# Two-layer block, MoE routing of the second layer placed inside the selective scan: one change to a Trainium2 kernel

## The chip, the cores and the metric

The kernel runs on one core of a Trainium2 chip. Its time is device microseconds of the execution, median of several runs. The core has a matrix engine (TensorE, PE in the profile, with PEld for its weight loads), VectorE (DVE), ScalarE (ACT), GpSimd (POOL), and SyncE (SP), which only issues transfers. Each engine works through its own instruction list in order and meets the others at semaphores; 16 DMA engines move the data. The profile counts from the start of the span of one profiled execution.

## What is computed

Two transformer-like layers on 4 batches of 1024 rows of 128 values (4096 tokens, float32). Layer 0 is causal attention and a mixture of experts; the change doesn't touch it. Layer 1 is a Mamba-style selective scan and a mixture of experts with a fixed capacity. The parts of layer 1 that matter here:

```python
# selective scan, per batch: over 1024 steps, 128 channels x 16 states
h = a_t * h + bu_t
y_t = jnp.einsum('bdn,bn->bd', h, c_t)

# experts, called once with every token's best expert and once with its second:
tpe = jnp.bincount(top_expert, length=NUM_EXPERTS)
indices = jnp.argsort(top_expert)
xe = jnp.where(valid[..., None], xf[tok_idx], 0.0)      # at most 512 tokens for each of 8 experts
h = jax.nn.gelu(jnp.einsum('ech,ehf->ecf', xe, w1), approximate=True)
ye = jnp.einsum('ecf,efh->ech', h, w2)
out = jnp.zeros((tokens + 1, hs), xf.dtype).at[tok_safe.reshape(-1)].add(ye.reshape(-1, hs))
```

Before each part the rows are layer-normalized and scaled and shifted by values made from a condition vector. Between the scan and the experts stand the norm, the scores (normed rows times an 128x8 router matrix), the choice of the best and of the second expert, and each token's slot: how many earlier tokens chose the same expert.

## The kernel before

Everything stays in SBUF as 32 tiles of 128 tokens; batch b owns tiles 8b to 8b+7 (`TPB` is 8). The stages of layer 1 are blocks of the program, one after the other, with a meeting of all engines between two blocks.

**The scan** (`selective_scan`) runs batch by batch. A batch has 16 groups of 8 channels; group (b, g) is a recurrence over 128 partitions and 1024 columns, done in two halves of 512. `scan_plan` writes one list of steps, and every engine walks through this one list in its order and does its own part of each step, so the list sets the order on all engines. For a group VectorE makes products in PSUM (`product`, `m_ps_bu`, L1993, twice) and two scans (`first_half` L2001, `second_half` L2007, both to `m_st`). ScalarE makes the decay `m_da` three groups ahead (L2153). GpSimd multiplies the state by C (`m_hc` or `attn_t`, L2171); the results stand in NHC = 8 buffers, and the states in 4 (`NST_BUF`). TensorE sums four groups at once (step `sum`, L1970 and L1973, queued two groups behind). SyncE brings the spread inputs (`m_x_rep`). Beside that, `prepare(b + 1)` puts the next batch's input steps (norm, turn, conv, u, z, raw, soft, rep, delta) beside groups 0 to 11 of batch b; the Silu steps load another table on ScalarE, and the step `table` (L2103) loads the first one again. The preceding batch's results are multiplied by z on GpSimd (L2183), put out and added to x beside groups 3 and 4 (step `out`, L1958, L1959, L2118), and their row statistics are made by VectorE beside groups 5 and 6 (step `stats`, L156, L160). Transposes and the like share two PSUM banks `ps_w`, in turn.

**The norm block** (`Norm`, "ln3") then normalizes all 32 tiles: GpSimd every fourth, VectorE the others, with scale and shift by rows as separate instructions (L212, L217, L219), TensorE transposes (L262) and makes the scores (L282), ScalarE copies (L229). Meanwhile SyncE loads the second layer's weights w2 and w1, 2 MB each (L2489, L2490).

**The experts' block** (`capacity_experts`) begins with `Dispatch`: on VectorE the choice of the best expert, running counts, slots, then the second expert and its slots and weights (L1111 to L1164), with two small TensorE products for the counts. GpSimd sends the 32 tiles of normed rows to their slots in DRAM by indirect DMAs (L2372), first all 32 of the first choice, then splits w1 into a high and a low part (`Split.gpsimd`, L305, 8 instructions, each after ScalarE's copy L299), then sends the 32 of the second. SyncE waits for all 32 sends of a choice and fetches expert after expert (L2393). TensorE handles 16 expert blocks (8 experts, two choices): transposes `c_tr`, L2262, products up (`c_up`) and down (`c_dn`, L2286). GpSimd gathers the results (L2383) once the 8 blocks of a choice are stored, and VectorE mixes them and adds them to x.

## Time and profile before

| | |
|---|---|
| Median of 3 runs | 1915.2 us (1911.8 to 1917.24) |
| Profiled execution | 1911.14 us, span of the core 1909.3 us |
| Busy over the span | PE 1554.6, DVE 1198.2, ACT 773.3, POOL 1264.3 us |
| Layer 0 | up to about 1371 us |
| Scan | 1371 to 1640.5 us |
| Norm block | 1640.8 to 1673.5 us |
| Experts' block | 1673.8 us to the end |

A row of a timeline is: start in us, duration in us, engine, line, operation, output<-inputs, shape, and how many instructions the row merges; brackets give the idle time before it and what ended it. A line is that of the kernel before. "issue" is time of no wait that the profile shows. The shares of busy time over the whole span say little here, since the change lies in three stages of the last 540 us.

### The profile page before, as it was taken

The numbers are of one execution on the slowest core, as the hardware profiler recorded it, in microseconds if no ns is written. First come the engines' busy times: TensorE is split into PE (matmuls) and PEld (weight loads), VectorE is DVE, ScalarE is ACT, GpSimd is POOL, SyncE is SP. The second block draws the span as 40 slices with busy tenths as digits, with TensorE's granted clock in tenths as the row PEclk, the third lists the DMA queues.
The fourth block names the chain that finished last, engine by engine and source line by source line (L and its number), as shares of the span: only waits on it lengthen the run. The fifth ranks groups of instructions, "written<-read, shape, count | busy, mean of one in ns | idle before, by whom it ended". The sixth has DMA issues, their size and how long they took to land. (4 is left out here: it accounts for less than half of the span.)

```text
span 1909.3 us, 26415 instructions
## 1 busy us (share of the span) xinstructions
PE 1554.6 (81%) x8848; PEld 1070.2 (56%) x8848; DVE 1198.2 (63%) x2522; ACT 773.3 (40%) x1294; POOL 1264.3 (66%) x1080
## 2 busy tenths in 40 slices
PE   5799999999999999999999999999875553517960
PEld 3455555756566665557566587888622211417850
DVE  6876676566666666765665065666589999732224
ACT  2245444354443454443444542322387663113320
POOL 5588898788887888987897842110047766368446
PEclk7799999999999999999999999999978777558985
DMA  6233221121213112211211020000065554213323
GB/s 174 67 78 84 62 67 34 45 67 36 65 36 78 34 40 62 68 34 45 67 42 26 13 63 1 1 1 1 24 165 145 147 151 119 91 38 105 97 65 86
DMA packets 93543, 125.29 MB, mean 66 GB/s; under 512 B 13648, under 2 KB 53476, under 8 KB 93408
## 3 DMA queue, kind: packets, MB, share of 16 engines
q1 hardware_dynamic: 89312, 115.58, 24.2%
q0 software_dynamic: 4096, 8.02, 1.5%
q8 instruction: 72, 1.18, 0.3%
q14 instruction: 63, 0.52, 0.1%
HBM read 56.56 MB, written 16.78 MB: 38 GB/s over the span
## 5 line engine op out<-in xcount | busy, mean ns | idle before, releaser
L835 DVE CUSTOM_DVE_ANT_0 ring<-ring,mask 128x128 f32<-128x128 f32 (+7 forms) x512 | 383.7, 769 | 185.3 <-PE ring L697 184.9
L921 ACT ACTIVATE prob<-ring 128x512 f32<-128x512 f32 x576 | 315.2, 598 | 297.0 <-PE ring L712 293.5
L975 POOL TENSOR_TENSOR acc<-acc,prob 128x512 f32<-128x512 f32 x272 | 353.1, 1298 | 72.8 <-ACT prob L921 48.9
L728 PE MATMUL ps_o<-prob,v 128*64 128x256 f32 x2304 | 281.5, 386 | 4.1 <-issue 3.8
L697 PE MATMUL ring<-k,x 128*128 128x512 f32 (+3 forms) x768 | 249.5, 404 | 37.7 <-ACT prob L921 22.1
L711 PE MATMUL ring<-x,k 128*128 128x512 f32 x576 | 257.7, 447 | 24.9 <-DVE neg_m L835 15.7
L712 PE MATMUL ring<-x,k 128*128 128x512 f32 x576 | 229.0, 398 | 0.0
L697 PEld LDWEIGHTS ring<-k,x 128*128 128x128 f32 x768 | 136.3, 197 | 145.1 <-ACT prob L921 50.5
L728 PEld LDWEIGHTS ps_o<-prob,v 128*64 128x64 f32 x2304 | 153.9, 136 | 106.0 <-issue 38.3
L972 POOL TENSOR_TENSOR acc<-prob 128x512 f32<-128x512 f32 x144 | 184.4, 1281 | 8.2 <-ACT prob L921 6.8
L942 POOL TENSOR_TENSOR other<-other,sin 128x512 f32<-128x512 f32 x96 | 136.3, 1420 | 58.4 <-DVE other L814 57.8
L711 PEld LDWEIGHTS ring<-x,k 128*128 128x128 f32 x576 | 109.2, 190 | 99.9 <-issue 43.6
L944 POOL TENSOR_TENSOR rot<-rot,other 128x512 f32<-128x512 f32 x96 | 129.2, 1346 | 7.5
L1681 POOL TENSOR_TENSOR first_h<-first_h,e_scaled 128x512 f32<-128x512 f32 x8 | 10.2, 1271 | 176.2 <-DVE e_scaled L1563 176.2
L712 PEld LDWEIGHTS ring<-x,k 128*128 128x128 f32 x576 | 109.8, 191 | 19.5 <-issue 6.9
L827 DVE TENSOR_TENSOR rot<-rot,other 128x512 fp32r<-128x512 f32 x64 | 73.1, 1142 | 69.5 <-ACT other L903 69.5
L1549 DVE TENSOR_TENSOR e_both<-e_silu,ps_moe 128x512 f32<-128x512 f32 x88 | 60.4, 686 | 87.1 <-PE ps_moe L1389 68.7
L2171 POOL TENSOR_TENSOR attn_t<-m_st,m_crep 128x1024 f32<-128x1024 f32 x32 | 75.3, 2358 | 55.8 <-DVE m_st L2007 49.0
L1633 ACT ACTIVATE e_silu<-ps_moe 128x512 f32<-128x512 f32 x88 | 52.6, 598 | 136.7 <-PE ps_moe L1389 133.9
L960 POOL TENSOR_SCALAR_AFFINE_SELECT prob<-prob 128x512 f32<-128x512 f32 x128 | 91.3, 713 | 24.8 <-ACT prob L921 23.7
L2383 POOL DMA_INDIRECT c_got<-slots_out,d_slot x64 | 64.8, 1012 | 63.1 <-DMA slots_out<-wo 44.2
L813 DVE TENSOR_TENSOR rot<-ring,cos 128x512 f32<-128x512 f32 x96 | 66.3, 690 | 59.2 <-PE ring L679 58.8
(301 smaller groups left out, 3050.8 us busy)
## 6 DMA issues: line engine op xcount, KB each, us to landing
x<-other SPq DMA_DIRECT2D x256, 128.0 KB, 2.4
m_x_rep<-u_mem SPq DMA_DIRECT2D x59, 512.0 KB, 4.6
x<-rot SPq DMA_DIRECT2D x128, 128.0 KB, 2.3
slots_in<-zeros SPq DMA_DIRECT2D x2, 2048.0 KB, 8.7
slots_out<-wo SPq DMA_DIRECT2D x16, 256.0 KB, 2.5
gate<-slots_in SPq DMA_DIRECT2D x11, 256.0 KB, 3.2
m_x_rep<-u_mem SPq DMA_DIRECT2D x10, 256.0 KB, 4.4
e_w<-in_w SPq DMA_DIRECT2D x3, 704.0 KB, 6.6
```

The source lines that it names most:

```text
L697: mm = e.matmul(ps[:, c0:c1], x1[g % 2][:, h, qs], k1[g % 3][:, c0:c1], start=True, stop=True)
L711: e.matmul(banks(step, BANK), k1[g % 3][:, ks], x1[g % 2][:, :, qs], start=True, stop=False)
L712: e.matmul(banks(step, BANK), k2[g % 3][:, ks], x2[g % 2][:, :, qs], start=False, stop=True).then_inc(s2_pe.sem, 1)
L728: mm = e.matmul(ps_o[s * D:(s + 1) * D, qb % 2 * 2 * P:(qb % 2 + 1) * 2 * P], v[g % 2][:, kb, :], prob[i % NPROB][:, s * 2 * P:(s + 1) * 2 ...
L835: e.tensor_tensor_reduce(ps, ps, mask_1[:, SEQ - n:SEQ], 1.0, -3.0 * NEG, ALU.add, ALU.min, neg_m[g % 2][:, c, h, qb % QPC:qb % QPC + 1]). ...
L921: e.activation(prob[i % NPROB][:, :], banks(("s2",) + key, BANK), ACT.Exp, scale=-1.0).then_inc(s2_exp.sem, 1)
L942: e.tensor_tensor(other[i][:, :], other[i][:, :], sin[:, cc], ALU.mult).then_inc(rotated.sem, 1)
L944: e.tensor_tensor(rot[i][:, :], rot[i][:, :], other[i][:, :], ALU.add).then_inc(rotated.sem, 1)
L960: e.affine_select(tile[:, :], tile[:, :], [[0, G], [1, P]], ALU.is_ge, 0.0, base=0, channel_multiplier=-1).then_inc(causal.sem, 1)
L972: e.tensor_tensor(total[:, :], first[:, :], tile[:, :], ALU.add).then_inc(summed.sem, 1)
L975: e.tensor_tensor(total[:, :], total[:, :], tile[:, :], ALU.add).then_inc(summed.sem, 1)
L2171: e.tensor_tensor(hc[(b * NG + g) % NHC][:, :], st[r][:, :], crep[b % 2][:, :], ALU.mult).then_inc(hc_pool.sem, 1)
```

## The change

The norm block is gone, and with it `Dispatch`. Its work up to the slots of the first choice is cut by batches and put as new steps into the scan's list (`routed`): batch b's statistics as before, then `rstd3` (two ACT, then five DVE instructions), `norm3` (ACT; scale and shift rows on POOL, for the last batch's first half on DVE), `turn3` and `score` (PE, ACT), `choose`, `count`, `place` (DVE, PE, DVE), beside the groups of batch b+1, and `send` (POOL), two tiles beside each of groups 2 to 5 of batch b+2. For batch 2 `count`, `place` and the sends come after the last group; for batch 3 all of it but the sends, which the experts' block begins with. The small DVE instructions are handed out one at a time between the big ones of a group (`between`); after the last group they go at once. `SecondChoice` does the second choice for all tokens at the experts' start. The loads of w1 (now two halves) and w2 are issued at the start of the experts' block. The `m_hc` buffers shrink from 8 to 6 since the normed rows `h` need the room, `h_t` holds two batches instead of four, and the zeroing of `c_got` moves to the second expert block.

```diff
+    def choose(self, e, b, scored):
+        c, shape, slots = self.chain, [P, TPB, NE], float(NE * CAPACITY)
+        sc, lead = self.scores[:, b * TPB:(b + 1) * TPB, :], self.less[:, b * TPB:(b + 1) * TPB, 0:NE]
+        e.wait_ge(*scored)
+        e.wait_ge(c.sem, c.n)
+        e.tensor_reduce(self.best[:, :], sc, AX, ALU.max).then_inc(c.sem, c.up())
...
+        yield
+
+        e.wait_ge(c.sem, c.n)
+        e.scalar_tensor_tensor(self.cand[:, :, :], lead, 0.0, each(self.no, shape), ALU.is_equal, ALU.add).then_inc(c.sem, c.up())
+        yield
...
+    def place(self, e, b, bank, counted):
+        c = self.chain
+        e.wait_ge(*counted)
+        e.wait_ge(c.sem, c.n)
...
-NHC = 2 * SET
+NHC = 6
...
-                plan.append(("out", b - 1, g - 3))
-            if b and g in (5, 6):
-                plan.append(("stats", b - 1, g - 5))
+            if (b, g) == (BATCH - 1, NG - 1):
+                plan.append(("end",))
+            for past in range(b):
+                plan += routed(past, (b - past - 1) * NG + g)
+    for at in range(NG, NG + 6):
+        plan += routed(BATCH - 2, at)
     while pend:
         summed()
-    for n in range(TPB // 4):
-        plan.append(("out", BATCH - 1, n))
-    for n in range(TPB // 4):
-        plan.append(("stats", BATCH - 1, n))
+    for at in range(NG + 6):
+        plan += routed(BATCH - 1, at)
     return plan
 
 
-LATER = 8
+def routed(b, at):
+
+
+    steps = {3: [("out", b, 0)], 4: [("out", b, 1)], 5: [("stats", b, 0)], 6: [("stats", b, 1), ("rstd3", b)],
+             9: [("norm3", b, 0)], 10: [("norm3", b, 1)], 11: [("turn3", b, 0)], 12: [("turn3", b, 1), ("score", b, 0)],
+             13: [("score", b, 1), ("choose", b)], NG: [("count", b), ("place", b)]}
+    if b < BATCH - 1:
+        for n in range(TPB // 2):
+            steps[NG + 2 + n] = [("send", b, 2 * n), ("send", b, 2 * n + 1)]
+    return steps.get(at, [])
+
...
+            small, ended = [], False
+
+            def between(steps=1):
+
+                while steps and small:
+                    if next(small[0], "none") == "none":
+                        small.pop(0)
+                    steps -= 1
+
             for step in plan:
                 kind, key = step[0], step[1:]
+                if kind == "end":
+                    ended = True
+                if kind == "rstd3":
+                    small.append(deviations3(e, *key))
+                elif kind == "choose":
+                    small.append(first.choose(e, *key, (act.sem, act.at["score", key[0], 1])))
+                elif kind == "place":
+                    small.append(first.place(e, *key, counts(ps_w[turn["count", key[0]] % NW]), (w_pe.sem, w_pe.at["count", key[0]])))
+                elif kind == "norm3" and not rows3_by(key)[1]:
+                    rows3(e, key, rows3_dve)
+                if ended:
+                    between(20)
                 if kind == "delta":
                     b, cc = key[0], part(key)
...
                         product(e, key, 0)
                     else:
                         product(e, key, 0)
+                        between()
                         second_half(e, behind(*key, 1))
+                    between()
                     first_half(e, key)
+                    between()
                     product(e, key, 1)
...
+        def deviations3(e, b):
+
+            ts, c = slice(b * TPB, (b + 1) * TPB), row_chain
+            r, t, var = rstd3[:, ts], nmr3[:, ts], mv[:, ts, 1]
+            e.wait_ge(rstd3_act, 2 * b + 2)
+            e.scalar_tensor_tensor(t, var, EPS, r, ALU.add, ALU.mult).then_inc(c.sem, c.up())
...
+                elif kind == "rstd3":
+                    b, = key
+                    ts = slice(b * TPB, (b + 1) * TPB)
+                    e.wait_ge(row_chain.sem, stats_at[b, 1])
+                    e.activation(log_var3[:, ts], mv[:, ts, 1], ACT.Ln, bias=eps[:, 0:1]).then_inc(rstd3_act, 1)
+                    e.wait_ge(rstd3_act, 2 * b + 1)
+                    e.activation(rstd3[:, ts], log_var3[:, ts], ACT.Exp, scale=-0.5).then_inc(rstd3_act, 1)
+                elif kind == "norm3":
+                    b, n = key
+                    e.wait_ge(nmr3_dve, b + 1)
+                    for j in range(4):
+                        i = b * TPB + 4 * n + j
+                        t = e.activation(h[:, i, :], x[:, i, :], ACT.Identity, bias=nmr3[:, i:i + 1], scale=rstd3[:, i:i + 1])
+                    t.then_inc(norm3_act.sem, 1)
+                elif kind == "turn3":
+                    if key != (0, 0):
+
+                        e.wait_ge(w_pe.sem, w_pe.at["score", (2 * key[0] + key[1] - 1) // 2, (2 * key[0] + key[1] - 1) % 2])
+                    e.activation(h3_t[:, :], bank[:, :], ACT.Copy).then_inc(act.sem, 1)
+                elif kind == "score":
+                    tile = key[0] * TPB + 4 * key[1]
...
         def vector(e):
-            slots.vector(e)
-            e.memset(got[:, :, :, :], 0.0).then_inc(got_zero, 1)
...
+                if n == 1:
+                    e.memset(got[:, :, :, :], 0.0).then_inc(got_zero, 1)
...
-                for i in range(TILES):
-                    e.indirect_dma_start(slots_in[k][:, :], bass.IndirectOffsetOnAxis(ap=slot[:, k, i:i + 1], axis=0), h[:, i, :], None,
-                                         bounds_check=NSLOT - 1, oob_is_err=False).then_inc(scattered[k], 16)
+            for i in range(TILES - TPB, TILES):
+                send(e, first, h, slots_in, 0, i, sent)
+            w_split.gpsimd(e)
+            e.wait_ge(second.slotted, 1)
+            for i in range(TILES):
+                send(e, first, h, slots_in, 1, i, scattered[1])
...
+            for half, (to, taken) in enumerate(w_from):
+                e.dma_start(to, a["w1_1"][half * E1 // 2:(half + 1) * E1 // 2, :, :].rearrange("e h f -> h e f")).then_inc(taken, 16)
+            e.dma_start(w2[:, :, :, :], a["w2_1"].rearrange("e (c f) n -> f e c n", f=P)).then_inc(consts_in[0], 16)
+            e.dma_start(bias_bc[:, :, :], a["bias"].to_broadcast([P, 1, HID])).then_inc(consts_in[0], 16)
             e.wait_ge(*consts_in)
```

The first place is VectorE's list in batch 1, around groups 13 to 15. `m_ps_bu` is a product, `m_st` a half of a scan, `f_...` are tiles of the new first choice. Before:

```order
L1993 TENSOR_TENSOR m_ps_bu<-m_x_rep,m_ps_b 128x512 x2
L2007 SCALAR_TENSOR_TENSOR m_st<-m_da,m_st,m_ps_bu 128x512
L2001 SCALAR_TENSOR_TENSOR m_st<-m_da,m_ps_bu 128x512
L1993 TENSOR_TENSOR m_ps_bu<-m_x_rep,m_ps_b 128x512 x2
L2007 SCALAR_TENSOR_TENSOR m_st<-m_da,m_st,m_ps_bu 128x512
```

After:

```order
L2125 TENSOR_TENSOR m_ps_bu<-m_x_rep,m_ps_b 128x512 x2
L1106 TENSOR_REDUCE f_best<-f_scores 128x8
L2139 SCALAR_TENSOR_TENSOR m_st<-m_da,m_st,m_ps_bu 128x512
L1109 TENSOR_TENSOR f_less<-f_scores,f_best 128x8x8
L2133 SCALAR_TENSOR_TENSOR m_st<-m_da,m_ps_bu 128x512
L1113 SCALAR_TENSOR_TENSOR f_cand<-f_less,f_no 128x64
L2125 TENSOR_TENSOR m_ps_bu<-m_x_rep,m_ps_b 128x512
L1116 TENSOR_REDUCE f_red<-f_cand 128x8
L2125 TENSOR_TENSOR m_ps_bu<-m_x_rep,m_ps_b 128x512
```

`f_best`, which waits for the scores, stands ahead of a half scan, and one small instruction follows each big one.

The second place is TensorE's list in batch 1, from the last input step (`rep`, to `m_ps_w` from `m_w_c`) over the sum of groups 8 to 11 (`m_ps_y`). Before:

```order
L1949 MATMUL m_ps_w<-m_u,m_w_c 128x512 x2
L1973 MATMUL m_ps_y<-attn_t,m_fold 32x512 x8
L1937 MATMUL m_ps_w<-ident,m_xn 128x128 x4
L1973 MATMUL m_ps_y<-m_hc,m_fold 32x512 x8
L1937 MATMUL m_ps_w<-ident,m_xn 128x128 x4
```

After:

```order
L2068 MATMUL m_ps_w<-m_u,m_w_c 128x512 x2
L2084 MATMUL m_ps_w<-ident,attn_t 128x128 x8
L2089 MATMUL m_ps_w<-m_gate,m_h_t 128x8 x4
L2105 MATMUL m_ps_y<-attn_t,m_fold 32x512 x2
L2105 MATMUL m_ps_y<-m_hc,m_fold 32x512 x2
L2105 MATMUL m_ps_y<-attn_t,m_fold 32x512 x2
L2105 MATMUL m_ps_y<-m_hc,m_fold 32x512 x2
L2089 MATMUL m_ps_w<-m_gate,m_h_t 128x8 x4
L2056 MATMUL m_ps_w<-ident,m_xn 128x128 x4
L1138 MATMUL m_ps_w<-f_mask,f_less_one 128x64
L1139 MATMUL m_ps_w<-f_upto,f_ones 128x64
```

The transposes of both halves and the first half's scores come ahead of the sum, the second half's scores behind it, and the two products of the step `count` behind the next batch's transposes.

The third place is GpSimd's list at the start of batch 2 (`wo` is the multiplication by z) and beside its middle. Before, groups 0 and 1, z, and groups 2 to 7:

```order
L2171 TENSOR_TENSOR attn_t<-m_st,m_crep 128x1024 x2
L2183 TENSOR_TENSOR wo<-wo,m_z 128x512 x2
L2171 TENSOR_TENSOR attn_t<-m_st,m_crep 128x1024 x2
L2171 TENSOR_TENSOR m_hc<-m_st,m_crep 128x1024 x4
```

After, from z to group 5, and then from group 9 to group 11:

```order
L2399 TENSOR_TENSOR wo<-wo,m_z 128x512 x2
L2382 TENSOR_TENSOR m_hc<-m_st,m_crep 128x1024
L1246 DMA slots_in<-attn_t,f_slot 4096x128 x2
L2382 TENSOR_TENSOR m_hc<-m_st,m_crep 128x1024
L1246 DMA slots_in<-attn_t,f_slot 4096x128 x2
L2382 TENSOR_TENSOR attn_t<-m_st,m_crep 128x1024
L1246 DMA slots_in<-attn_t,f_slot 4096x128 x2
L2382 TENSOR_TENSOR attn_t<-m_st,m_crep 128x1024
L1246 DMA slots_in<-attn_t,f_slot 4096x128 x2
```

```order
L2382 TENSOR_TENSOR m_hc<-m_st,m_crep 128x1024 x4
L2248 TENSOR_TENSOR attn_t<-attn_t,rows_bc 128x512
L2250 TENSOR_TENSOR attn_t<-attn_t,rows_bc 128x512
L2382 TENSOR_TENSOR attn_t<-m_st,m_crep 128x1024
L2392 TENSOR_TENSOR m_brep<-m_brep,m_delta 128x1024
L2248 TENSOR_TENSOR attn_t<-attn_t,rows_bc 128x512
L2250 TENSOR_TENSOR attn_t<-attn_t,rows_bc 128x512
L2382 TENSOR_TENSOR attn_t<-m_st,m_crep 128x1024
```

Eight sends stand between the groups' multiplications, and later two pairs of row multiplications and additions around the one of `m_brep`.

## Rows read from the trace of the kernel before

**Rows 1.** The chain that ended last, by engine and line (page).

```profile
POOL slots_in L2372 3%; POOL c_got L2383 2%; PE c_dn L2286 1%; DMA c_got<-slots_out,d_slot 0%; DMA slots_out<-wo 0%; PE c_up L2274 0%; PE c_up L2275 0%; PE c_up L2276 0%; DMA c_rows<-slots_in 0%; DMA slots_in<-attn_t,d_slot 0%; ACT wo L2352 0%; POOLq L2372 0%; DVE c_got L2317 0%; POOLq L2416 0%; POOLq L2383 0%
```

**Rows 2.** Windows: busy us (count) mean of PE, PEld, DVE, ACT, POOL; clock; DMA.

```profile
1560.00:1580.00 20.00, 7.15 (x32) 1.20 (x32) 19.93 (x24) 8.81 (x9) 14.10 (x7) 0.59 0.60 157
...
1700.00:1720.00 20.00, 0.00 (x0) 0.00 (x0) 0.00 (x0) 0.00 (x0) 15.33 (x16) 0.50 0.14 49
```

**Rows 3.** Timeline: end of the scan, last statistics, split, first expert, second sends.

```profile
1627.68 1.28 DVE L2007 TENSOR_TENSOR_SCAN m_st<-m_da,m_st,m_ps_bu 128x512 f32<-128x512 f32 x1
...
1640.16 0.38 DVE L160 BATCH_NORM_AGGREGATE mv<-stats 128x2 f32<-128x6 f32 x4
...
1722.76 9.84 POOL L305 TENSOR_TENSOR w_1lo<-w,w_1hi 128x512 fp32r<-128x512 f32 x8
...
1727.06 1.11 PE L2262 MATMUL c_tr<-ident,gate 128*128 128x128 f32 x4 [41.28 <-DMA gate<-slots_in]
...
1772.38 0.97 POOL L2372 DMA_INDIRECT slots_in<-attn_t,d_slot  x1 [0.30 <-issue]
...
1777.35 0.66 PE L2262 MATMUL c_tr<-ident,c_rows 128*128 128x128 f32 x4 [1.62 <-DMA c_rows<-slots_in]
```

**Rows 4.** Timeline, DVE: a group's second half, and the next group's.

```profile
1480.06 1.27 DVE L2007 TENSOR_TENSOR_SCAN m_st<-m_da,m_st,m_ps_bu 128x512 f32<-128x512 f32 x1
...
1483.54 1.27 DVE L2007 TENSOR_TENSOR_SCAN m_st<-m_da,m_st,m_ps_bu 128x512 f32<-128x512 f32 x1
```

**Rows 5.** Timeline, DVE and POOL: instructions with two SBUF inputs beside POOL's.

```profile
1221.21 1.27 POOL L1681 TENSOR_TENSOR first_h<-first_h,e_scaled 128x512 f32<-128x512 f32 x1 [12.17 <-DVE e_scaled L1563]
...
1221.69 0.94 DVE L1427 SCALAR_TENSOR_TENSOR e_cand<-e_less,e_no 128x128 f32<-128x128 f32 x1
...
1222.98 0.29 DVE L1431 TENSOR_TENSOR e_mask<-e_yes,e_red 128x128 f32<-128x128 f32 x1
```

**Rows 6.** Timeline, DVE and ACT: statistics and table loads beside groups 5 to 7.

```profile
1475.54 0.38 DVE L160 BATCH_NORM_AGGREGATE mv<-stats 128x2 f32<-128x6 f32 x4
1480.06 1.28 ACT L2103 ACT_TABLE_LOAD   x1
...
1535.83 0.38 DVE L160 BATCH_NORM_AGGREGATE mv<-stats 128x2 f32<-128x6 f32 x4
1538.81 1.28 ACT L2103 ACT_TABLE_LOAD   x1
...
1372.84 0.30 ACT L2069 ACTIVATE m_log_var<-mv,eps 128x24 f32<-128x24 f32 x1
```

**Rows 7.** Timeline, POOL: a group, z, the product for the next batch.

```profile
1481.41 2.35 POOL L2171 TENSOR_TENSOR m_hc<-m_st,m_crep 128x1024 f32<-128x1024 f32 x1 [1.12 <-DVE m_st L2007]
...
1520.62 2.51 POOL L2183 TENSOR_TENSOR wo<-wo,m_z 128x512 f32<-128x512 f32 x2
...
1556.13 2.35 POOL L2176 TENSOR_TENSOR m_brep<-m_brep,m_delta 128x1024 f32<-128x1024 f32 x1
```

**Rows 8.** Timeline, PE and ACT: transposes, scores, copies, norms, a sum.

```profile
1657.96 1.37 PE L262 MATMUL ps_ln<-ident,attn_t 128*128 128x128 f32 x4
1659.13 1.72 PE L282 MATMUL ps_route<-gate,attn_t 128*128 128x8 f32 x8
1659.37 0.60 ACT L229 ACTIVATE attn_t<-ps_ln 128x512 f32<-128x512 f32 x1 [2.14 <-PE ps_ln L262]
...
1518.31 1.64 ACT L2084 ACTIVATE m_xn<-first_h,m_nmr,m_rstd 128x128 f32<-128x128 f32 x4
...
1439.33 3.64 PE L1973 MATMUL m_ps_y<-attn_t,m_fold 128*32 128x512 f32 x16 [7.78 <-POOL attn_t L2171]
```

**Rows 9.** Timeline, SP: the issue of the first experts' fetch.

```profile
1724.05 0.93 SPq L2393 DMA_DIRECT2D gate<-slots_in  x2
```

**Rows 10.** The line of w1's load: time to landing.

```profile
DMA to landing us min/median/max: 15.3/15.3/15.3
```

**Rows 11.** Timeline, POOL: the slowest gathers, beside VectorE's mixing.

```profile
1884.10 1.15 POOL L2383 DMA_INDIRECT c_got<-slots_out,d_slot  x1 [0.30 <-issue]
```

345 lines of the change are left out of this document (220 added, 125 removed).

## The prediction

> **What bounds the kernel now.** I read the chain that ended last first: its share on the sends (POOL slots_in) and on the gathers is 3% and 2%, small, since most of the chain is layer 0 and the scan [rows 1]. So the rest is read stage by stage. In the scan VectorE is busy 19.93 of 20 us: every instruction added to it, and every wait in it, lengthens the span [rows 2]. Between the scan's last state at 1628.96 (1627.68 + 1.28) and the first transpose of an expert at 1727.06 lie 98.1 us in which TensorE does next to nothing: in 1700 to 1720 it has no instruction at all, VectorE none either, and GpSimd issues 16 sends in 20 us; the wait ahead of that transpose is 41.28 us, for a fetch that waits for all 32 sends [rows 2, 3]. From 1727.06 to the end at 1909.3 are 182.2 us of experts and gathers. The change shortens the 98.1 and pays in the scan. Three terms, then.
>
> **Term 1: the gap.** After the last state there remain:
> - product with C, sum, z, put out, statistics: today 1628.96 to 1640.54, 11.6 us [rows 3]; unchanged.
> - `rstd3`: 0.6 for two ACT steps (0.30 each [rows 6]); five small dependent VectorE steps at 0.23, 1.2. Thus the deviations are there at +13.4.
> - `norm3`: 1.64 for four tiles on ACT [rows 8], twice: +15.0 and +16.6. Row instructions of the second half on GpSimd, whose sends of batch 2 (8 x 1.28 from +3) end before that: 2 of 1.27, the length of a 128x512 product there [rows 5], +19.3.
> - transposes of that half 1.37, +20.7; scores of the first half, which stand behind them, 1.5, +22.2 (8 matmuls took 1.72, [rows 8]); their copy, needed as the banks are two, some 0.6 as the one in [rows 8]; scores and copy of the second half, +25.0.
> - seven small steps of the choice 1.6, count (two matmuls) 1.5, place 1.3, the meeting 0.35: 29.75.
>
> Nothing covers these: all engines wait for one batch. Then, from the block's start, SyncE first issues 4 MB of weights. Before, the two loads were issued one behind the other as well, and w1 had landed 15.3 after its issue [rows 10]; with the first one's issue and the bias it is some 17 us from the first issue. SyncE waits for them ahead of the first fetch. The last 8 sends need 8 x 1.28 = 10.2 (0.97 + 0.30 each [rows 3]) and are covered by that. The fetch took 1727.06 - 1724.05 = 3.0 [rows 3, 9]. First transpose: block start + 20. Sum of the gap: 29.75 + 20 = 49.75, against 98.1: **-48.35 us**. The w1 split (9.84 us, [rows 3]) lies on GpSimd behind the 8 sends, ends at +20.5 and covers the second choice (about 17 us on VectorE); it stays in place.
>
> **Term 2: the experts.** They wait a little for the second sends in their middle: the rest of the 32 after the split end at block start + 20.5 + 41 = 61.5, that is 41.5 after the first transpose; before, 1772.38 + 0.97 - 1727.06 = 46.3. The 1.62 us for which TensorE waited there go [rows 3]: **-1.6 us**. Else the 182.2 stay, since 16 blocks on TensorE, the storing and 64 gathers are as before.
>
> **Term 3: the scan.** A group's cycle on VectorE is 3.48 us (1480.06 to 1483.54), without a gap [rows 4].
> (a) Issue: 49 small instructions, 18 for each of batches 0 and 1 and 13 of batch 2, that lie between big ones. Four aggregates of statistics take 0.38 together [rows 3], some 0.1 each; the new ones, 8 to 128 wide, mostly follow a big one on which they don't depend: an estimate of 0.07 to 0.13 each, by width, 5.2 in all, with 0 and 10 as its bounds.
> (b) Waits for GpSimd. A VectorE instruction with two SBUF inputs that started at 1221.69 beside a GpSimd one (1221.21 + 1.27 = 1222.48) took 0.94 and ended at 1222.63, behind its end, where one of the same shape at 1222.98, beside nothing, took 0.29 [rows 5]. In the scan GpSimd is busy 2.35 of 3.48, idle 1.12 [rows 7]; the small instructions with two SBUF inputs (`cand`, the carry, one of `place`, the five deviations) fall at random into that: a hit costs up to 2.35, a miss nothing. 12.5 in all: `cand` 1.2 and carry 0.6 in three batches, 5.4; `place` 1.1; deviations 0.6, 1.2, 4.2 in batches 1, 2, 3. Bounds 0 and about 25.
> (c) Deviations: VectorE's first waits for ACT's `rstd3`, and that stands in ACT's list behind the Silu steps. In batch 1 the statistics end at 1475.92, VectorE comes there 0.7 later, 1476.6, but the table load that ACT must pass ends at 1481.34, then 0.5: wait 5.3. In batch 2 the statistics end at 1536.21 and the load at 1540.09 [rows 6]; GpSimd's sends push the latter by 4.3 to 1544.9 (by way of the sum and the input steps queued behind it on TensorE), place and its wait push VectorE to 1539.8: 5.0. In batch 3 no Silu step stands ahead: 0.1. Sum 10.4. This wait holds all products and scans.
> (d) Scores. Let t be the end of group 9's last scan. In batches 1 and 2 GpSimd then has: product with C 2.35; rows of half 0, 2.5; product of group 10, 2.35; `m_brep`, 2.35 [rows 7]; rows of half 1, 2.5: +12.2. Transposes 1.37 [rows 8], +13.4; ACT copy and half 0's scores +15.1; then the sum of groups 8 to 11 stands ahead of half 1's scores: 3.64 when the clock is low (1439.33, [rows 8]) less what has run by then, +17.4; scores and copy, +18.65. VectorE comes to `best` after three groups (10.44) and 2.3 of a fourth, t + 12.73. It waits 5.9. In batch 3, with no `m_brep`, 3.6. Sum 15.4. Behind the wait stand the group's second half scan and all after it, and GpSimd, which has no state to work on.
> (e) `count` stands on TensorE behind the next batch's transposes: `place` waits 2.1 in batch 2.
> Sends: 8 x 1.28 = 10.2 in batches 2 and 3 on GpSimd. With z, 2.51 [rows 7], that is 12.7 by group 5, less 3.0 by which VectorE itself comes later (the wait and the small steps of `place`) and 5.3 of its room: it is 4.4 us behind VectorE there. The 4 states and 6 products allow 8.1, so VectorE doesn't stall.
> Term 3: 5.2 + 12.5 + 10.4 + 15.4 + 2.1 = **+45.6 us**. The last state would stand at 1674.6.
>
> **Sum.** 1909.3 - 48.35 - 1.6 + 45.6 = 1905.0 us span. The profiled execution's own time is 1911.14 for 1909.3, and the median 1915.2 is 4 above it; the change of -4.3 is taken from the median: 1910.9, **1911 us**. That is 0.2% less, below the 0.3% that a measurement of this kernel can tell from no change. Its own range, 1903 to 1919: (c) and (d) can each err by 4.
>
> **Rivals.**
> R1, the gap counts and the scan's waits are mostly not there. (c) and (d) hang on the positions in four lists, each known to a microsecond or two, and I let every engine be as late as it can. If the two are half as long (14.0 with (e)) and a small step meets GpSimd seldom (5 for 12.5), the scan grows by 5.2 + 5 + 14 = 24.2: 1889.5. With no waits left, 17.7: 1883. For it: GpSimd's idle 1.12 in each group [rows 7], in which the order may settle, as VectorE then starts behind it; against: the table loads' place is fixed by the list.
> R2, the slower side: sends in the scan take longer beside a full VectorE. Each then costs 1.28 + d. The backlog, 4.4 + 8d, passes the 8.1 of room from d = 0.46 on, and VectorE stalls for the rest in batches 2 and 3, 2 x (8d - 3.7); the last eight, beside the end of the scan, hold the last row instructions by 8d - 3.4. At d = 1: 8.6 + 4.6 = 13.2, 1924 us; it passes 1915 from d = 0.63. Against: gathers beside VectorE's mixing took at most 1.15 where sends beside nothing took 0.97, d = 0.2 [rows 3, 11]; for: VectorE there was not at 100%.
> The Trainium skill (SBUF — State Buffer, "SBUF: two separate sides") knows of such a lock: VectorE in its two-port mode keeps GpSimd from writing a DMA's descriptors, and a transfer that takes some 620 ns alone takes some 3100 ns. An estimate by that page: d = 2.5 and, by R2's sum, 1960. The same page ("Who interferes with whom") doesn't count products with an input in PSUM or SBUF among those operations (inferred there), and no row here shows sends beside a scan.
> R3, the first fetch comes late: weights beside sends land slower, or something else that SyncE passes; 8 us more give 1919. The 15.3 is beside no sends [rows 10].
> R4, the waits in the scan are longer than I count, since (c) to (e) feed each other through the 3-deep chain of ACT's decays: +8 more, 1919, counted with the forecast's upper side.
>
> **Chances.** Forecast (1903 to 1919) 0.47, R1 0.28, R2 0.13, R3 and R4 beyond 1919 0.12. Faster than 1909.5 takes R1 and a third of the forecast's own range: 0.43; slower than 1921 R2 and half of the last: 0.18; between 0.39. Range 1884 to 1927, from R1's end to R2's with d a little over 1.
>
> **What would show it.** Expected in the changed profile: first transpose of an expert near 1724; scan ending near 1674; idle ahead of `f_best` of 5.9, 5.9 and 3.6 us, released by ACT's score copy; idle ahead of the first deviation of 5 us in batches 1 and 2, released by ACT; `f_cand` at 1 us or more on average instead of 0.2; sends in the scan at 1.3 us each; the scan's end to the first transpose 49.75 us. If VectorE has no idle time in the scan, R1 holds; if sends stand at 2 us and idle time of VectorE lies at groups 5 to 8 of batches 2 and 3, R2. I'd be wrong altogether if the experts' 182.2 us changed by more than 3, since nothing in them was costed but the second sends.

## The result, and the profile after

The changed kernel takes 1917.35 us (median of 12 runs), the kernel before 1912.48 (12 runs); the ratio is 1.0022, with a 95% interval of 1.0013 to 1.0030. So it is slower by 4.9 us in the medians (0.13 to 0.30% by the interval), where I had forecast 4.3 us less. The profiled run's span is 1915.8 us, 6.5 more than that of the profiled run before; the stages below are read from these two.

The end of the scan and the start of the experts in the kernel after, to be set beside [rows 3] (a timeline, columns as there; L2139 is the second half of a scan, L1106 and L1163 the first and last step of the choice, L2618 the issue of w1's load, L2479 an expert's transpose):

```profile
1680.62 1.28 DVE L2139 TENSOR_TENSOR_SCAN m_st<-m_da,m_st,m_ps_bu 128x512 f32<-128x512 f32 x1
...
1694.21 0.38 DVE L160 BATCH_NORM_AGGREGATE mv<-stats 128x2 f32<-128x6 f32 x4
...
1707.77 0.22 DVE L1106 TENSOR_REDUCE f_best<-f_scores 128x8 f32<-128x64 f32 x1 [8.47 <-ACT f_scores L2311]
...
1712.06 0.17 DVE L1163 TENSOR_TENSOR f_slot<-f_late,f_base 128x8 int32<-128x8 f32 x1
...
1712.50 0.94 SPq L2618 DMA_DIRECT2D w<-in_w  x2
...
1731.91 1.11 PE L2479 MATMUL c_tr<-ident,gate 128*128 128x128 f32 x4 [13.04 <-DMA gate<-slots_in]
```

The last state is there at 1681.90, 52.9 us later than before (forecast 45.6). From it to the first transpose are 50.0 us (forecast 49.75, before 98.1). From there to the end are 183.9 (forecast 180.6, before 182.2). The gap came out as worked out to 0.3 us; the scan cost 7.3 us more than I had, the experts 3.3. Of the 52.9 us, 0.4 stand ahead of the scan: its first half scan begins at 1392.46, before at 1392.03. From that to the last state are 289.4 us (289.6 in e13, a second trace of the same kernel), and before 236.9 (236.9 in e16).

VectorE's idle times in the scan of the kernel after (same view; all over 1.1 us; they are the figures in brackets):

```profile
1482.62 0.17 DVE L2229 SCALAR_TENSOR_TENSOR m_nmr<-mv,m_rstd 128x8 f32<-128x8 f32 x1 [5.45 <-ACT m_rstd L2296]
...
1517.42 0.22 DVE L1106 TENSOR_REDUCE f_best<-f_scores 128x8 f32<-128x64 f32 x1 [6.94 <-ACT f_scores L2311]
...
1532.77 0.23 DVE L1150 TENSOR_TENSOR f_prod<-m_ps_w,f_mask 128x64 f32<-128x64 f32 x1 [1.40 <-PE m_ps_w L1139]
...
1562.88 0.17 DVE L2229 SCALAR_TENSOR_TENSOR m_nmr<-mv,m_rstd 128x8 f32<-128x8 f32 x1 [5.09 <-ACT m_rstd L2296]
...
1598.87 0.22 DVE L1106 TENSOR_REDUCE f_best<-f_scores 128x8 f32<-128x64 f32 x1 [8.12 <-ACT f_scores L2311]
...
1670.98 0.22 DVE L1106 TENSOR_REDUCE f_best<-f_scores 128x8 f32<-128x64 f32 x1 [4.39 <-ACT f_scores L2311]
```

The waits stand at the places that the prediction named: two for the deviations (5.45 and 5.09, forecast 5.3 and 5.0), three for the scores (6.94, 8.12, 4.39, forecast 5.9, 5.9, 3.6), one for the count (1.40, forecast 2.1). Together 31.4 us. The other 21.5 of the 52.9 are the small instructions themselves and what they wait for inside. Such a wait doesn't show as idle time: the instruction is recorded as running, and is long. Twelve of them are; here are two of the choice in batch 1, with `f_red`, a short one, between them and `f_base` again at the end of the scan, then GpSimd's two products beside the long ones:

```profile
1520.00 1.34 DVE L1113 SCALAR_TENSOR_TENSOR f_cand<-f_less,f_no 128x64 f32<-128x64 f32 x1
...
1521.86 0.20 DVE L1116 TENSOR_REDUCE f_red<-f_cand 128x8 f32<-128x64 f32 x1
...
1525.20 1.23 DVE L1126 TENSOR_SCALAR f_base<-f_red 128x8 f32<-128x8 f32 x1
...
1709.31 0.15 DVE L1126 TENSOR_SCALAR f_base<-f_red 128x8 f32<-128x8 f32 x1
```

```profile
1518.91 2.34 POOL L2382 TENSOR_TENSOR m_hc<-m_st,m_crep 128x1024 f32<-128x1024 f32 x1 [4.08 <-DVE m_st L2139]
...
1524.06 2.34 POOL L2382 TENSOR_TENSOR attn_t<-m_st,m_crep 128x1024 f32<-128x1024 f32 x1 [2.81 <-DVE m_st L2139]
```

`f_cand` ends at 1521.34, behind the end of GpSimd's product at 1521.25. `f_base` reads one small tensor and still takes 1.23 us and ends at 1526.43, behind GpSimd's next product (1526.40), where at the end of the scan, with GpSimd idle, it takes 0.15. The twelve are 17.4 us long instead of some 2.2: 15.2 us of waiting, and some 6 remain for the issue of all 49.

Two more places. Sends in the scan, one of the first and one of the last of batch 0's, go at the rate that they had in [rows 3]:

```profile
1548.15 0.99 POOL L1246 DMA_INDIRECT slots_in<-attn_t,f_slot  x1 [0.30 <-issue]
...
1557.83 0.97 POOL L1246 DMA_INDIRECT slots_in<-attn_t,f_slot  x1 [0.31 <-issue]
```

And in the experts' block a 128x32 product takes 8.28 us, beside GpSimd's split of w1 (it ends at 1733.27, the split's eight instructions at 1733.19), and the second transpose waits 3.34 us where it waited 1.60 before (all from the timeline of after):

```profile
1723.39 9.80 POOL L305 TENSOR_TENSOR w_1lo<-w,w_1hi 128x512 fp32r<-128x512 f32 x8
...
1735.66 0.99 POOL L1246 DMA_INDIRECT slots_in<-attn_t,f_slot  x1 [2.47 <-DVE f_slot L1241]
```

```profile
1724.99 8.28 DVE L1230 TENSOR_TENSOR d_weight<-d_weight,d_ex 128x32 f32<-128x32 f32 x1
```

```profile
1736.36 1.09 PE L2479 MATMUL c_tr<-ident,gate 128*128 128x128 f32 x4 [3.34 <-DVE c_xt_lo L2525]
```

### The profile page after: what moved, and what is told of

Read it like the earlier page. It is cut to its first block and busy times, and to the rows that moved or that the text cites. A ratio compares the mean times of both kernels' runs of the same rounds, so it can differ in the third digit from the quotient of the medians.

```text
span 1915.8 us, 26497 instructions
## 1 busy us (share of the span) xinstructions
PE 1559.0 (81%) x8866; PEld 1074.2 (56%) x8866; DVE 1204.3 (63%) x2514; ACT 784.9 (41%) x1339; POOL 1272.6 (66%) x1071
## 5 line engine op out<-in xcount | busy, mean ns | idle before, releaser
L835 DVE CUSTOM_DVE_ANT_0 ring<-ring,mask 128x128 f32<-128x128 f32 (+7 forms) x512 | 383.6, 769 | 183.6 <-PE ring L697 183.1
L711 PE MATMUL ring<-x,k 128*128 128x512 f32 x576 | 258.0, 448 | 24.7 <-DVE neg_m L835 15.4
L2382 POOL TENSOR_TENSOR m_hc<-m_st,m_crep 128x1024 f32<-128x1024 f32 x42 | 98.9, 2355 | 63.7 <-DVE m_st L2139 57.1
L2599 POOL DMA_INDIRECT c_got<-slots_out,f_slot x64 | 66.0, 1031 | 64.8 <-DMA slots_out<-wo 45.9
```

The costliest lines, as they stand in the source:

```text
L711: e.matmul(banks(step, BANK), k1[g % 3][:, ks], x1[g % 2][:, :, qs], start=True, stop=False)
L835: e.tensor_tensor_reduce(ps, ps, mask_1[:, SEQ - n:SEQ], 1.0, -3.0 * NEG, ALU.add, ALU.min, neg_m[g % 2][:, c, h, qb % QPC:qb % QPC + 1]). ...
L2382: e.tensor_tensor(hc[(b * NG + g) % NHC][:, :], st[r][:, :], crep[b % 2][:, :], ALU.mult).then_inc(hc_pool.sem, 1)
L2599: e.indirect_dma_start(got[:, k, i, :], None, slots_out[k][:, :], bass.IndirectOffsetOnAxis(ap=slot[:, k, i:i + 1], axis=0), bounds_check= ...
```

## The experiments

e1 to e4 ran on one chip, e5 to e8 on a second, e9 to e12 on a third, e13 to e16 on a fourth. On the second and third the kernel before itself takes 1962 and 1963 us, so times are compared only within a chip, or by their ratio to the kernel before. VectorE's waits in the scan of the unedited changed kernel (after, e9, e13) agree to 0.1 us, and so do those of e6, which is edited in the experts alone. Where the scan begins varies by up to 6 us between the runs (1389.8 to 1396.2), whatever the kernel. "After" is the changed kernel in its first comparison. A "place" is one of the four points of a group at which one small VectorE instruction is handed out: ahead of and behind the second half scan, behind the first half scan, and behind the second product.

**e1: fewer buffers, before.** One edit in the kernel before.

```diff
-NHC = 2 * SET
+NHC = 6
```

> The kernel before with one edit: 6 instead of 8 buffers for the product with C. Theory A (the buffers cost nothing, as the prediction has it): the time of the kernel before, ratio 0.999 to 1.001. Rival (the six buffers make GpSimd wait for TensorE's sums and carry part of the 4.9 us by which the changed kernel is slower): 1.001 to 1.003, with idle time of GpSimd ahead of products with C that PE's sums release, and idle time of VectorE in the scan.

Ratio 1.0002 (0.9993 to 1.0012), no new idle time on VectorE in the scan, and none of GpSimd that TensorE's sums end. The six buffers cost nothing by themselves.

**e2: the choice two groups later.**

```diff
-             13: [("score", b, 1), ("choose", b)], NG: [("count", b), ("place", b)]}
+             13: [("score", b, 1)], 15: [("choose", b)], NG + 2: [("count", b), ("place", b)]}
...
-            steps[NG + 2 + n] = [("send", b, 2 * n), ("send", b, 2 * n + 1)]
+            steps[NG + 4 + n] = [("send", b, 2 * n), ("send", b, 2 * n + 1)]
```

> The changed kernel with the step choose two groups later, and count, place and the sends behind it, two groups later as well. Theory A (VectorE's waits ahead of the first step of the choice, 6.94, 8.12 and 4.39 us in the trace of after, are a matter of the place in the list alone): two groups are 7 us, so about 18 of the 19.5 us go: span near 1898, ratio to before about 0.993. Rival (the waits come from GpSimd and ScalarE running behind, and VectorE's wait only lets them catch up, so that it comes back elsewhere): less than 6 us go, ratio 0.999 or more, with new idle time of VectorE ahead of products or scans.

Ratio 0.9917 (0.9902 to 0.9932), span 1892.8 us. The last state is at 1657.44 instead of 1681.90, but some of the wait moved on. VectorE in batch 2 of e2:

```profile
1590.18 0.22 DVE L1106 TENSOR_REDUCE f_best<-f_scores 128x8 f32<-128x64 f32 x1 [0.16 <-ACT f_scores L2311]
1593.17 0.70 DVE L2125 TENSOR_TENSOR m_ps_bu<-m_x_rep,m_ps_b 128x512 f32<-128x512 f32 x1 [2.77 <-ACT m_ps_b L2347]
```

8.12 became 0.16, and a wait for ScalarE's copy at the next batch's start, absent there in after, is 2.77. Two such waits (2.17 a batch earlier) and a 2.7 us longer gap (the last sum now stood behind batch 2's count on TensorE) are in the result; even so about 20 us went by moving the choice and what follows it two groups down the list, somewhat more than the 18 expected. Theory A stands for the waits: they are a matter of the place in the list. But the 20 us are not those waits alone. The third of them (4.39) and the eight small steps of batch 2's choice went behind the last state, into the longer gap; the second wait for the deviations fell from 5.09 to 2.27; and the long small instructions left in the scan take 11.0 us, not 17.4.

**e3: the deviations two groups later.** ScalarE's two steps stay; VectorE takes its five with a new step at 8.

```diff
-6: [("stats", b, 1), ("rstd3", b)],
+6: [("stats", b, 1), ("rstd3", b)], 8: [("dev3", b)],
...
-                if kind == "rstd3":
+                if kind == "dev3":
                     small.append(deviations3(e, *key))
```

> The changed kernel with VectorE's five deviation steps handed out two groups later (ScalarE's two steps stay). Theory A: the waits of 5.45 and 5.09 us ahead of them go and the norms start at most 2 us later, so that the waits for the scores grow by 0 to 4 us in sum: 6 to 10 us less, ratio 0.997 to 0.999. Rival (the wait moves on to the scores, whose chain begins with these steps): the waits for the scores grow by 8 us or more, ratio 1.001 to 1.003.

Ratio 0.9978 (0.9968 to 0.9988), as expected: 0.44% below after's. Both waits are gone, and the waits for the scores are 8.08, 7.84 and 4.64, 1.1 us more in sum. But now two small instructions meet GpSimd worse (3.69 and, a batch later, 3.39 us). VectorE of e3 in batch 2, and GpSimd there:

```profile
1560.22 3.69 DVE L2229 SCALAR_TENSOR_TENSOR m_nmr<-mv,m_rstd 128x8 f32<-128x8 f32 x1
```

```profile
1559.21 4.67 POOL L2382 TENSOR_TENSOR m_hc<-m_st,m_crep 128x1024 f32<-128x1024 f32 x2
```

The first ends at 1563.91, behind both products of GpSimd (1563.88): it does not get in between two that follow each other.

**e4: no small instruction behind the first half.**

```diff
                     first_half(e, key)
-                    between()
```

> The changed kernel with no small VectorE instruction between a first half scan and the product behind it (three places in a group instead of four). Theory A (in this place GpSimd's product with C is under way, and a small instruction with two inputs in SBUF, or a TENSOR_SCALAR from SBUF to SBUF, ends only when that ends; ten such of 1.24 to 1.36 us instead of about 0.2 in the trace of after): 10 times 1.1 go, less 1 to 4 for a choice that ends later and makes count wait: 7 to 10 us less, ratio 0.997 to 0.999, and no small instruction over 0.5 us while GpSimd keeps up. Rival (the small ones meet GpSimd wherever they are): the long ones turn up in the other places, ratio 1.001 to 1.003.

Ratio 1.0000 (0.9991 to 1.0010), some 4 us less than after by the ratios, where I expected 7 to 10. The long ones turned up in the next place, as the rival had it. VectorE of e4 in batch 1:

```profile
1519.80 0.76 DVE L1113 SCALAR_TENSOR_TENSOR f_cand<-f_less,f_no 128x64 f32<-128x64 f32 x1
...
1524.23 0.81 DVE L1123 TENSOR_TENSOR_SCAN f_upto<-f_keep,f_mask 128x64 f32<-128x64 f32 x1
...
1526.79 1.88 DVE L1130 TENSOR_TENSOR f_carry<-f_carry,f_upto 128x8 f32<-128x8 f32 x1
```

Between the two products (1519.80) GpSimd still has 0.7 us to go, 1518.13 + 2.35 = 1520.48, and `f_cand` ends at 1520.56. So theory A's forecast, that nothing over 0.5 us would be left, failed: 14 are. It named the place too narrowly. That a small instruction ends only when GpSimd's product does, which both theories have, holds in these rows too.

**e5: every small instruction one place later.** An empty step ahead of each string, which moves all kinds through the places.

```diff
+        yield
         e.wait_ge(*scored)
```

> The changed kernel with one empty step ahead of every string of small VectorE instructions, so that each stands one place later in the group than in after, and nothing else. Theory A (an instruction ends late only if it has two inputs in SBUF or is a TENSOR_SCALAR from SBUF to SBUF, and only while GpSimd's product runs): behind the first half now stand f_less and f_upto, 1.2 us each, while f_rank, a TENSOR_REDUCE, which stands there too, stays at 0.3 us or less; f_cand, f_base and f_late, one place later, take 0.7. Rival (the place alone does it): f_rank takes 1.2 us there too. Time within 4 us of the changed kernel.

One execution, on the second chip. VectorE of e5 at the start of batch 2, and GpSimd's product, which runs to 1533.55:

```profile
1532.46 0.25 DVE L1155 TENSOR_REDUCE f_rank<-f_prod 128x8 f32<-128x64 f32 x1
1532.62 0.69 DVE L2127 TENSOR_TENSOR m_ps_bu<-m_x_rep,m_ps_b 128x512 f32<-128x512 f32 x1
1533.22 0.36 DVE L1159 TENSOR_SCALAR f_late<-f_rank 128x8 f32<-128x8 f32 x1
```

```profile
1531.19 2.36 POOL L2385 TENSOR_TENSOR m_hc<-m_st,m_crep 128x1024 f32<-128x1024 f32 x1 [1.99 <-issue]
```

A TENSOR_REDUCE, now behind the first half, and a product with one input in PSUM pass beside GpSimd; the TENSOR_SCALAR ends at 1533.58, with GpSimd. In after the same `f_late` stood behind the first half and took 1.31. `f_upto` (two inputs in SBUF) takes 1.40 there now, as expected. `f_less` takes 0.20, not 1.2 us: after the wait for the scores GpSimd had nothing to do. Theory A on the kinds is shown, and the rival, that the place alone does it, is out. What I had expected of the time, within 4 us of the changed kernel, did not come: the scan is 11.6 us shorter than in after (277.9 instead of 289.4), since the deviations are asked for a place later (waits 4.08 and 3.87), the count no longer waits, and fewer small ones meet GpSimd (seven long ones, 11.1 us).

**e6, e10, e14: the mixing weights later.** The three steps for the weights move behind the second expert block's evictions.

```diff
                 if n == 1:
+                    second.weights(e)
                     e.memset(got[:, :, :, :], 0.0).then_inc(got_zero, 1)
```

> The changed kernel with the three VectorE steps for the mixing weights (sum, reciprocal, product) moved from within the second choice to behind the second expert block's evictions. Theory A (the product d_weight, 8.28 us in the trace of after beside GpSimd's eight split instructions, holds VectorE's first evictions and the second choice's slots): the second transpose of an expert comes 1.7 us or more sooner after the first, the second sends start 2 us sooner, and 1.8 to 3.3 us of time go: ratio to before 1.0005 to 1.0013. Rival (the split of w1, not this, sets the first products): nothing moves, 1.0022.

> The kernel of e6 beside the unedited changed kernel. Theory A (d_weight's 8.28 us beside the split hold the first evictions): against e9 1.5 to 3.5 us less, ratio to e9 0.9982 to 0.9992, and the experts stage from the first transpose on 181 to 182.5 us instead of 183.9. Rival (another limit takes its place): within 1 us of e9.

> The kernel of e6 and e10. Theory A (d_weight beside the split of w1 holds the first evictions and the second choice's slots): on a chip like that of e1 to e4 the experts' stage takes 181 to 182.5 us, ratio to e13 0.9982 to 0.9992. Rival (the stage is set by something behind it, as the gathers of the second choice): stage 183.5 or more, within 1 us of e13.

e6 gave 1.0060 (1.0043 to 1.0077), and e10 1.0042 (1.0027 to 1.0057) beside e9's 1.0044: nothing can be read from these times, since another thing takes some 50 us in that stage on their chips (below), though in both the second transpose waits 1.60 us, and 3.85 in e9. On the fourth chip e14 is 1.0018 (1.0009 to 1.0027) beside 1.0023 (1.0012 to 1.0034) for e13; the intervals overlap, and the medians, 1915.44 and 1916.53, are 1.1 apart. The rows tell more. The second transpose, in e13 and then in e14:

```profile
1733.81 1.09 PE L2479 MATMUL c_tr<-ident,gate 128*128 128x128 f32 x4 [3.25 <-DVE c_xt_lo L2525]
```

```profile
1733.56 1.09 PE L2482 MATMUL c_tr<-ident,gate 128*128 128x128 f32 x4 [1.60 <-DVE c_xt_lo L2528]
```

From the first transpose (1729.44 in e13, 1730.84 in e14) to the end are 183.1 us in e13 and 181.5 in e14. 1.65 us of TensorE's wait is what d_weight costs; the stage is shorter by as much, and the effect on the time is too small to be shown by the medians.

**e7: three small ones together ahead of the second half, one behind it, none elsewhere.**

```diff
-                        between()
+                        between(3)
                         second_half(e, behind(*key, 1))
-                    between()
+                        between()
                     first_half(e, key)
-                    between()
                     product(e, key, 1)
-                    between()
```

> The changed kernel with the four places for small VectorE instructions in a group changed to three together ahead of the second half scan, and one behind it; none behind the first half and none behind the second product. Theory A (GpSimd's product with C runs from the second half's end for 2.35 us, so only the stretch just ahead of the next second half is free of it): no small instruction over 0.5 us in batches 1 and 2, and 9 to 13 us less than the changed kernel, ratio 0.9955 to 0.9975. Rival (GpSimd runs behind often enough that the small ones meet it anywhere): 4 us less or nothing, ratio 1.000 or more.

1964.46 us, ratio 1.0019 (1.0010 to 1.0029), on the chip of e6, whose scan is after's: 8.1 us less than e6's 1972.55, a little under the 9 to 13 expected, and its last state is at 1675.6, 6.7 sooner. (The ratio expected, 0.9955 to 0.9975, counts from after's 1.0022; here e6 stands at 1.0060.) In batches 0 to 2 nothing over 0.5 us is left; two stay long in batch 3, where GpSimd is behind with its sends. The first of them with the one ahead of it, and GpSimd beside them in e7:

```profile
1632.01 0.17 DVE L2227 SCALAR_TENSOR_TENSOR m_nmr<-mv,m_rstd 128x8 f32<-128x8 f32 x1
1632.21 2.92 DVE L2230 TENSOR_TENSOR m_nmr<-m_nmr,m_rstd 128x8 f32<-128x8 f32 x1
```

```profile
1631.74 0.98 POOL L1246 DMA_INDIRECT slots_in<-attn_t,f_slot  x1 [0.30 <-issue]
1632.72 2.38 POOL L2380 TENSOR_TENSOR m_hc<-m_st,m_crep 128x1024 f32<-128x1024 f32 x1
```

It began during a send, was not through when that ended, and waited for the product behind it as well. That the send itself holds such an instruction is not shown: the one ahead of it, with two inputs in SBUF too, began within the same send and took 0.17. The gain in VectorE's own time was 8.7 us (the 6.7 and 2.1 more of waits); those 2.1 went back to the waits for the scores (7.64, 8.35, 5.54), since GpSimd's row steps, on which they hang, came no sooner.

**e11: the second half's scores ahead of the sum.**

```diff
-12: [("turn3", b, 1), ("score", b, 0)],
-             13: [("score", b, 1), ("choose", b)],
+12: [("turn3", b, 1), ("score", b, 0), ("score", b, 1)],
+             13: [("choose", b)],
```

> The changed kernel with the second half's scores on TensorE ahead of the sum of groups 8 to 11 instead of behind it (that sum took 3.2 us in the trace of after, at the low clock, between the two). Theory A (the sum is 2.5 to 3 us of each wait for the scores): the three waits fall to about 4.2, 5.4 and 1.7 us, together 8 us less: ratio to e9 0.995 to 0.997. Rival (the copies on ScalarE, which share one buffer, set the scores): the waits fall by less than 1 us each.

The waits for the scores fall to 5.43, 6.20 and 2.86, by 4.9 in sum, and one for the deviations grows from 5.10 to 6.59. The scan is 3.5 us shorter; the ratio, 1.0041 (1.0025 to 1.0056), cannot be told from e9's 1.0044 (1.0029 to 1.0060). Between the two theories: the sum carries 1.5 to 1.9 us of each wait, not 2.5 to 3, since the second half's scores now wait 0.84 for ScalarE's copy. TensorE in e11:

```profile
1510.03 1.71 PE L2089 MATMUL m_ps_w<-m_gate,m_h_t 128*128 128x8 f32 x8
1512.58 1.85 PE L2089 MATMUL m_ps_w<-m_gate,m_h_t 128*128 128x8 f32 x8 [0.84 <-ACT f_scores L2311]
```

**e8, e12, e15: the edits together.** e8 is e2, e3, e6 and e7, with the last sum ahead of batch 2's count and the last batch's row steps on VectorE. e12 and e15 are one kernel: e8 with e11 and with the first fetch issued without the wait for w2 and the bias, which TensorE and VectorE wait for instead.

> The changed kernel with the edits of e2, e3, e6 and e7 together, with batch 2's count, place and sends behind the last sum (in e2 they stood ahead of it and the stretch from the last state to the first transpose of an expert was 2.7 us longer), and the last batch's row instructions all on VectorE. Theory A (the costs add): from e2's span of 1892.8, less 7 for the deviations' waits, 8 for the meetings with GpSimd, 2.5 for the weights, 2.7 for the sum: span 1872, ratio 0.977 to 0.982. Rival (GpSimd, with some 58 us of work in a batch, becomes the bound as VectorE's waits go): over 1882, ratio 0.984 or more, with VectorE's idle time ahead of scans or products.

> The kernel of e8 with e11's order and with the first fetch issued without a wait for w2 and the bias (TensorE and VectorE wait for those themselves, later). Theory A: e8 had a last state at 1650.0 and 50.9 us from there to the first transpose; the fetch is issued 4 us sooner, as its last send lands, and the experts' stage takes 182: span 1650 + 47 + 182 = 1879 on a chip like the first, ratio to before 0.980 to 0.984. Rival (the fetch waits for the sends or the split of w1 comes last): no gain over e8, 0.984 to 0.987.

> The kernel of e12. Theory A (the edits add and the chip made up the rest): on a chip like that of e1 to e4 the span is 1649 + 48 + 182 = 1879, ratio to before 0.980 to 0.984. Rival (what the scan gave is lost in the experts' stage): ratio 0.987 or more, as on the chip of e12.

e8: 0.9864 (0.9848 to 0.9881); e12: 0.9873 (0.9858 to 0.9888); e15: 0.9854 (0.9841 to 0.9868), 1885.44 us against 1911.88 on its chip. So the idea of the change, with its steps put elsewhere in the list, is 26 us faster than the kernel before. Each is less than I expected (0.977 to 0.982 for e8, 0.980 to 0.984 for e12 and e15): e8 and e12 came out where their rivals were or beside it, e15 between the two. In e15's trace the last state is at 1653.9, 5 us later than I put it, the gap is 51.7, not 48, and the experts' stage 181.8. The 5 us are not the scan's: it begins at 1395.87, in e12 at 1391.04, and takes 258.0 us in e15 and 257.7 in e12. Three more things are in the rows. VectorE waits 3.21 for a count in batch 2. Six small instructions in the scan are long (8.1 us, the longest 2.24 beside GpSimd), where e7 has two. And the first fetch came hardly sooner, 16.0 us behind w1's issue, where after has 16.5: the wait that I took out was not what held it. SyncE's waits in e15 name what did, the landing of the last eight sends:

```profile
SPq L2616 <- DMA slots_in<-attn_t,f_slot: 3.5, 1, 3.5
```

In after the same wait is 3.6 us and ends at 1728.5, and the bias, the last load, follows 0.5 later. The two end together there, so taking out one of them gives next to nothing.

**e9, e13, e16: the two kernels unedited on further chips.**

> The changed kernel itself, unedited, as the measure for the other kernels on this chip. Both theories: ratio to before 1.001 to 1.004 if the chip is like the first; on a chip like that of e5 to e8 1.002 to 1.006, since their experts stage took 233 us instead of 184 with TensorE waiting for instructions.

> The changed kernel itself as the measure for the others on this chip. On a chip like that of e1 to e4: ratio to before 1.002, experts' stage 183.9 us. On one like that of e5 to e12: 1.004 to 1.006, stage 233 to 237 us.

> The kernel before. On a chip like that of e1 to e4 its stages stand as in the first trace: last state at 1629, first transpose at 1727, end at 1909. On one like that of e5 to e12: Theory A (TensorE's instructions come late there in the experts' stage, whatever the kernel): the same last state and first transpose within 3 us, and 230 us for the stage, with some 35 us of TensorE's idle time put down to issue. Rival (the changed kernels alone have it): 182 us.

e9: 1.0044 (1.0029 to 1.0060); e13: 1.0023 (1.0012 to 1.0034), as in the first comparison. e16's span is 1910.2 us, with the last state at 1628.7 and the first transpose at 1726.7: the experts' stage takes 183.5 in it and 182.2 in the first trace of before. That stage varies by 1.3 us between two runs of one kernel, nearly as much as was in question. Since e16's chip was like the first, its expectation for the other kind of chip stayed untested.

What e9's chip does in the experts' stage, by windows of 40 us (columns: busy us of PE, PEld, DVE, ACT, POOL, each with its count; granted clock, DMA share, GB/s), e9 and then e13:

```profile
1740.00:1780.00 40.00, 18.90 (x80) 13.90 (x80) 10.19 (x6) 4.10 (x4) 30.55 (x32) 0.67 0.15 51
```

```profile
1740.00:1780.00 40.00, 40.00 (x286) 36.95 (x285) 14.88 (x13) 15.74 (x18) 25.75 (x27) 1.00 0.37 110
```

And TensorE's timeline of e9 in it:

```profile
1753.45 0.38 PE L2479 MATMUL c_tr<-ident,gate 128*128 128x128 f32 x2 [1.15 <-issue]
...
1758.44 0.59 PE L2492 MATMUL c_up<-c_xt_lo,w_1hi 128*128 128x512 f32 x1 [1.69 <-issue]
```

TensorE stands for 38.5 us in 25 pieces that no data or engine ends. The same holds in all of e5 to e12 (31.6 to 41.4 us). The unedited kernel's gap is longer there as well, 54.3 us in e9 where after has 50.0; that of e12 is not (51.0, in e15 51.7). There is no trace of the kernel before from them; its time there, 1962, says that it has this too, or something of its size. What it is stays open. Late instructions would look like this; so might something from outside this core, and on the page of each of these eight runs, and of no other, the chain that ended last puts 2% of the span to "another core or an unknown queue".

## Why the prediction was wrong

The forecast was 4.3 us less, and it is 4.9 us more; the time lies inside the stated range and the sign is wrong. The sum held two terms of 48 and 46 us with opposite signs, and the second was off by 16%. The step that failed is term 3, the scan: 45.6 forecast, 52.9 measured. In it (d), the waits for the scores, was 4.05 us short, because the sum on TensorE had not begun when I let it have run in part; and (b), the waits for GpSimd, was short because I had left TENSOR_SCALAR out. Term 2 failed besides, by 3.3. In spans the three terms make up the 10.8 us between 1905.0 and 1915.8; some of that is what a profiled run differs by from the median.

- **The gap: right.** 50.0 against 49.75, with its parts: statistics end at +12.7 (forecast 11.6), slots at +30.3 (29.4), first transpose 19.4 behind w1's issue (20). One step in it held with little to spare: the last eight sends were to be covered by the weights, but their landing at 1728.5 ended only 0.5 us ahead of the bias's, and in e15 it alone sets the fetch.
- **(c) deviations: right** to 0.2 us each. ScalarE's list and the table load set it. e3 shows that they cost what they last.
- **(d) scores: mechanism right, size low** by 4.05 us. In batch 1 GpSimd's last row step ended at t + 12.4, where I had 12.2; then the sum of groups 8 to 11 took 3.2 us (1512.88 to 1516.10, below) and had not begun earlier, where I had counted 2.3 on the thought that part of it had already run. In batch 2 GpSimd's row steps come 1 us later on top, as they wait 1.03 for ScalarE's norm. e11 puts 1.5 to 1.9 us of each wait on the sum.

```profile
1512.88 1.07 PE L2105 MATMUL m_ps_y<-attn_t,m_fold 128*32 128x512 f32 x2
...
1516.10 1.06 PE L2089 MATMUL m_ps_w<-m_gate,m_h_t 128*128 128x8 f32 x8
```

- **(e) count: high** by 0.7.
- **(a) and (b), small instructions: low** by 3.8, and for a reason that I had excluded. I let only instructions with two SBUF inputs wait for GpSimd. Seven TENSOR_SCALARs with one small SBUF input took 1.23 to 1.36 us; they make 8 of the 15.2 us of waiting, while `f_carry` and `place`'s additions, which I had charged, met nothing. The two errors partly cancel. Nor do the small ones fall at random into GpSimd's busy time, as (b) has it: the place decides, and with other places e7 takes all but two of the long ones away. The Trainium skill (SBUF — State Buffer, "Who interferes with whom") names `tensor_scalar` among those that can take the pair of ports shared with GpSimd, and `tensor_reduce` as one that on this chip never contends; the rows of after and of e5 agree with both (1.31 against 0.25 behind the first half). I had read the section for the sends and not for this.
- **The experts: the gain of 1.6 us came, and was eaten.** TensorE's wait for the second sends is gone from the trace of after, as forecast, but ahead of the second transpose it waits 1.74 us more, for d_weight. I wrote that the split covers the second choice. It doesn't cover it; it blocks it, by the very rule of (b), which I applied in the scan alone. e14 puts it at 1.65 us of TensorE's wait, and its stage of 181.5 is 0.9 from the 180.6 forecast. The rest of the 3.3 is not explained; the stage of one kernel varies by 0.8 (after, e13) to 1.3 us (before, e16).
- **R1** (the waits shrink to half) is out: they came to 31.4 us, where the forecast had 27.9. **R2** (sends beside a full VectorE slow down) is out: 0.97 to 1.01 us each but for the first, 1.23. **R3** is out: the first transpose stands 19.4 behind w1's issue. **R4**, waits longer than counted, is the nearest to what came, if not by its cause: I had it at +8, and the span is 10.8 above the 1905.0 of the sum.

The chances were the second fault. By the bounds that the prediction set (faster below 1909.5, slower above 1921), 1917.35 lies between, which had 0.39. But a forecast of -4 made of two opposite terms near 47, of which one rests on five waits worked out, says little on the sign; "faster" should not have been at 0.43 with "slower" at 0.18. R1 says that I let every engine be as late as it can. In two places I did not: the sum counted as partly run, and TENSOR_SCALARs counted as free of GpSimd.

## What to carry to other kernels

When work is moved into a loop whose bound engine has no idle time, find the step's position by when its input is ready in every list it passes, then add slack: moving the choice down by two groups gave back 20 us here (e2), against two new waits of 2.2 and 2.8 us and a gap longer by 2.7. A tiny instruction between large ones is priced by what the neighbour sharing its ports does at that moment, not by its size. And where a change trades two large terms, give the sign little trust unless the terms are known better than their difference.

## What the hardware showed that I had not expected

- A 128x32 product with two inputs in SBUF took 8.28 us beside eight GpSimd instructions in a row, and an 8-wide one 3.69 beside two: such a VectorE instruction, once waiting, gets no turn between GpSimd instructions that follow without a gap. In e7 one that began during a send ended only with the product behind it, though the one ahead of it passed beside the same send in 0.17.
- TENSOR_SCALAR with one SBUF input of 8 values a partition waits like one with two inputs (1.23 to 1.36 us against 0.15); TENSOR_REDUCE doesn't (0.25 in e5's row, and 0.42 for the wider d_sum beside the split in after).
- Two of the four chips of the experiments ran, in all eight traces from them, the experts' stage in 232 to 237 us instead of 183, at the same scan, with 32 to 41 us of TensorE's idle time put down to nothing. A few tenths of a per cent can't be compared between such chips.
